# One quarter of an MLP's first activation moved to Pool, four instead of two banks of its second activation on the vector engine

## The reference

```python
f   = lrelu(conv(x, sw1)); f = lrelu(conv(f, sw2)); f = conv(f, sw3)      # 16 features
h   = lrelu(conv(concat[f, pts[d]], mw1) + mb1)     # 17 -> 32
h   = lrelu(conv(h, mw2) + mb2)                     # 32 -> 32
h   = lrelu(conv(h, mw3) + mb3)                     # 32 -> 16
sdf = sigmoid(conv(h, mw4) + mb4)                   # 16 -> 1
x   = x1 + sdf
```

## Time and profile before

| | us |
|---|---|
| median of 3 runs | 9322.48 |
| lowest and highest | 9307.45, 9324.88 |
| span of the profiled execution | 9326.0 |
| PE, DVE, ACT, POOL busy | 8848.9, 8762.5, 8085.3, 5789.8 |

### The profile page before, as it was taken

The page is one execution under the profiler, slowest core; times in us unless marked ns, Lnnn a source line. Parts: engine busy times, 40 slices in busy tenths (PEclk is TensorE's granted clock), DMA queues, the critical chain, the costliest instruction groups (busy, mean ns, idle before and its releaser), DMA issues. The chain is left out here.

```text
span 9326.0 us, 448546 instructions
## 1 busy us (share of the span) xinstructions
PE 8848.9 (95%) x199690; PEld 3696.6 (40%) x199690; DVE 8762.5 (94%) x9984; ACT 8085.3 (87%) x12777; POOL 5789.8 (62%) x2583
## 2 busy tenths in 40 slices
PE   7999999999999999999999999899999999999999
PEld 4555555555555555555555555311111111111111
DVE  6999999999999999999999999899999999999998
ACT  6888888888887888888888888699999999999999
POOL 6999999999999999999999999400000000000000
PEclk9999999999999999999999999899999999999999
DMA  4333333333333333333333333211111111111110
GB/s 116 98 94 90 85 82 87 99 99 95 85 83 83 96 94 96 86 88 77 87 88 83 87 84 82 58 32 32 34 34 32 32 31 32 34 32 32 34 34 19
DMA packets 394249, 638.98 MB, mean 69 GB/s; under 512 B 98016, under 2 KB 98626, under 8 KB 391810
## 3 DMA queue, kind: packets, MB, share of 16 engines
q1 hardware_dynamic: 389184, 608.56, 25.1%
q10 hardware_dynamic: 2498, 0.95, 0.0%
q0 software_dynamic: 640, 0.77, 0.0%
HBM read 270.15 MB, written 71.30 MB: 37 GB/s over the span
## 5 line engine op out<-in xcount | busy, mean ns | idle before, releaser
L1087 DVE TENSOR_TENSOR_SCAN arena<-arena,carried,ps 128x512 f32<-128x512 f32 x3968 | 4758.3, 1260 | 284.9 <-PE ps L505 271.4
L934 POOL TENSOR_TENSOR arena<-arena 128x1024 f32<-128x1024 f32 x2048 | 4799.9, 2394 | 89.8 <-PE ps L516 35.4
L1152 DVE SCALAR_TENSOR_TENSOR arena<-arena,neg_p 128x512 f32<-128x512 f32 x4096 | 2748.1, 744 | 0.1
L804 ACT ACTIVATE arena<-arena,a_neg 128x512 f32<-128x512 f32 x4096 | 2662.3, 710 | 15.7 <-DVE arena L1087 8.9
L505 PE MATMUL ps<-arena 64*32 64x128 f32 x131072 | 2306.2, 275 | 71.9 <-DVE arena L1087 41.7
L505 PEld LDWEIGHTS ps<-arena 64*32 64x32 f32 x131072 | 1848.2, 106 | 1197.1 <-DVE arena L1087 666.4
L873 ACT ACTIVATE arena<-ps,b2t 128x1024 f32<-128x1024 f32 (+1 forms) x2048 | 2076.2, 1077 | 201.1 <-PE ps L637 193.7
L637 PE MATMUL ps<-arena,w2s 32*32 32x512 f32 x32768 | 1549.3, 600 | 115.2 <-ACT arena L873 102.9
L879 ACT ACTIVATE arena<-ps,bm 128x1024 f32<-128x1024 f32 x1024 | 1165.6, 1138 | 2.0 <-PE ps L648 2.0
L648 PE MATMUL ps<-arena,m 64*32 64x512 f32 x16384 | 1127.4, 600 | 3.3 <-ACT arena L879 0.9
L516 PE MATMUL ps<-arena,sel 128*32 128x512 f32 x8192 | 1012.1, 611 | 66.5 <-POOL arena L934 60.9
(11 more groups left out here) (138 smaller groups left out, 5738.2 us busy)
## 6 DMA issues: line engine op xcount, KB each, us to landing
arena<-arena SPq DMA_DIRECT2D x4096, 64.0 KB, 2.4
arena<-c_d SPq DMA_DIRECT2D x1024, 128.0 KB, 3.3
xr<-in_x SPq DMA_DIRECT2D x128, 256.0 KB, 3.2
x_d<-xr SPq DMA_DIRECT2D x128, 256.0 KB, 3.3
xs<-x_d SPq DMA_DIRECT2D x128, 256.0 KB, 4.2
xr<-x_d SPq DMA_DIRECT2D x128, 256.0 KB, 3.7
out<-arena SPq DMA_DIRECT2D x128, 256.0 KB, 2.4
xs<-in_x SPq DMA_DIRECT2D x96, 256.0 KB, 3.2
```

The lines of the kernel that those rows point to most:

```text
L804: A(dA[(UNITS * t + m) % DR][:, gi, :], drep[:, e, :], ACT.Exp, scale=a_neg[:, e, 2 * gp + gi:2 * gp + gi + 1]).then_inc(s_dA, 1)
L934: nc.gpsimd.tensor_tensor(hc[m % CR], H[:, m % HR, :, :], crep[:, 2 * gp:2 * gp + 2, :], ALU.mult).then_inc(s_ch, 1)
L1087: V.tensor_tensor_scan(H[:, m % HR, gi, :], dA[(UNITS * t + m) % DR][:, gi, :], dbu[m % 2].rearrange("p (l g) -> p g l", g=2)[:, gi, :], 0 ...
L1152: m = V.scalar_tensor_tensor(out=t1[k % 4][:, q, :], in0=g[par], scalar=neg_p[:, i:i + 1], in1=gs_[par], op0=ALU.max, op1=ALU.add)
```

## The change

In each step, the t1 tile of q = 3 is made by Pool in place of DVE. Pool does it with two instructions: a tensor_scalar (min with the largest finite float, which changes nothing, then max with -p) from g into one of two new tiles `top`, and a tensor_tensor that adds gs into t1. Pool writes them in the order maximum(j), add_slope(j - 1). maximum(j) waits for the end of add_slope(j - 2), which stands just ahead of it in the queue; add_slope waits for its maximum and for the t1 buffer. mm2 waits for Pool's semaphore as well. SHARED grows from (1, 3) to (0, 2, 4, 6): DVE makes bank 3 of the second activation in four steps of eight and ACT in the other four. The loop of DVE in `leaky1` shrinks from four to three instructions, and `spread_g` waits for Pool's last use of the g and gs buffers.

```diff
-SHARED = (1, 3)
+SHARED = (0, 2, 4, 6)
+HUGE = 3.4028234663852886e38
...
+        top = [over(50 + i, 1) for i in range(2)]
...
-        pool_counts = {s_du: 1, s_dg: 2, s_ch: UNITS}
+        pool_counts = {s_du: 1, s_dg: 2, s_ch: UNITS, s_top: NG, s_l1p: NG}
...
             def mm2(t, k):
                 pe.wait_ge(s_l1, t * NG + (k + 1))
+                pe.wait_ge(s_l1p, t * NG + (k + 1))
...
+            def maximum(n, k):
+                t, s, par = n + 1, n // 4 + 1, n // 4 % 2
+                pool.wait_ge(s_l1p, t * NG + k - 1)
+                if n % 4 == 0 and k == 0:
+                    pool.wait_ge(s_g, s + 1)
+                i = GQ * (NG * (n % 4) + k) + GQ - 1
+                nc.gpsimd.tensor_scalar(top[k % 2], g[par], HUGE, neg_p[:, i:i + 1], ALU.min, ALU.max).then_inc(s_top, 1)
+
+            def add_slope(n, k):
+                t, par = n + 1, n // 4 % 2
+                pool.wait_ge(s_top, t * NG + k + 1)
+                pool.wait_ge(s_m2, t * (2 * NG) + 2 * (k - 3))
+                nc.gpsimd.tensor_tensor(t1[k % 4][:, GQ - 1, :], top[k % 2], gs_[par], ALU.add).then_inc(s_l1p, 1)
...
             for n in range(0, NT):
                 layer0(n)
+            for j in range(NG * NT + 1):
+                if j < NG * NT:
+                    maximum(j // NG, j % NG)
+                if j > 0:
+                    add_slope((j - 1) // NG, (j - 1) % NG)
...
             def spread_g(s, par):
 
                 dve.wait_ge(s_gp, s + 1)
+                if s > 2:
+                    dve.wait_ge(s_l1p, NG * (4 * (s - 2) + 1))
...
-                for q in range(GQ):
+                for q in range(GQ - 1):
```

More of the change, by code:

```diff
@@ L197, in mamba_sdf_kernel @@
         s_l1, s_m2 = sem("s_h1"), sem("s_mm2")
+        s_top, s_l1p = sem("s_h1_maximum_by_pool"), sem("s_h1_by_pool")
         s_t2, s_m3 = sem("s_h2"), sem("s_mm3")
```

## The result

The changed kernel takes 10,250.7 us (10,248.0 to 10,252.7, 4 runs) against 9323.4 us before. The ratio is 1.0997, 95% interval 1.0983 to 1.1011. The loss is 927 us where 1267 us were predicted.

The account below looks back on a forecast made before the run. It took PE, DVE and ACT, coupled in layer 1 at 3.265 us a step, as the bound. DVE 2.43 plus Pool 2.00 gave 4.43, 4.5 with wake-ups; times 1024 steps, 1265 us more, 10,590 us; range 10,130 to 11,250.

Parts of the forecast that it names:

- What bounds the kernel: Layer 1, 3.265 us a step: PE, DVE and ACT coupled; relieving one gains a few per cent, no more.
- Removed and added: Layer 1, per block of 8 steps: DVE nets 2.4 us freed of 26.1, ACT loses 0.84 us; PE keeps its matmuls.
- Exclusion: Layer 1: DVE instructions with two SBUF operands and Pool instructions reading SBUF exclude each other; 4.43 us a step.
- A run keeps the other out: From layer 0's trace: a back-to-back Pool run holds DVE out for the whole run, 4.07 us, not one instruction's 2.39.
- The sum: Layer 1 step: DVE 2.43 plus Pool 2.00 makes 4.43 us, 4.5 by the two-step walk; 10,590 us, 13.6% slower.
- wake-ups: Layer 1: restart delays of Pool, PE and DVE, estimated at 0.35 us in all for two steps.
- Pool's pair: Layer 1, each step: Pool's tensor_scalar 0.80 us and tensor_tensor 1.20 us, together 2.0 us.
- a walk: Two steps of layer 1: DVE burst 4.7, Pool pair 2.0, mm2 and L1161 1.95, 0.35 more: 9.0 us.
- The fast rival: Layer 1: long DVE and Pool instructions stream side by side, ACT sets the pace; middle 9,170 us; chance 0.05.
- Pool far slower: Layer 1: Pool's min-max takes 2.4 us, making the step 6.0 us, 12,150 us; chance 0.06.
- The clock: Layer 1: longer PE gaps drop the clock to 1.2 GHz, PE's work doubles to 5.4 us, 11,510 us; chance 0.04.
- Signs listed: Layer 1: 4.5 us steps, single L1152 of 2 us and more, longer Pool instructions, PE at 7 tenths, L1161 waiting longer.

Follow-up runs that it names:

- e12: Changed kernel with g read from its PSUM bank, first two feature layers in mm4's bank, SHARED back to (1, 3): 9349.2 us, ratio 1.0022 to before.
- e10: Kernel before with g read from its PSUM bank and first two feature layers in mm4's bank, no Pool work: 9331.0 us, ratio 1.0004.
- e2: Kernel before with only SHARED changed to (0, 2, 4, 6), Pool doing nothing in layer 1: 9578.2 us, ratio 1.027.
- e1: Changed kernel with SHARED put back to (1, 3), Pool still making its quarter: 9914.6 us, ratio 1.0632 to before.
- e3: Kernel before, DVE making all four tiles, with Pool's two instructions a step added into scratch tiles nobody reads: 10,632.5 us, ratio 1.1405.
- e4: As e3, with Pool's two instructions replaced by two memsets that only write SBUF: 9326.0 us, ratio 1.0 to before.
- e6: Changed kernel with features computed once, for the first four blocks, and g in SBUF: 10,185.7 us, ratio 1.0924 to before.
- e7: As e6, but DVE's first-activation instruction reads g from PSUM instead of SBUF: 9098.5 us, ratio 0.9756 to before.
- e9: Changed kernel, whole computation, g read from its PSUM bank by DVE, first two feature layers in mm4's bank: 9254.2 us, ratio 0.9926 to before.

## Why the prediction came out as it did

**What bounds the kernel.** Borne out by e12 against e10, and by e2: DVE, ACT and PE run in one period. Taking DVE's load away alone gains nothing, adding to it costs 250 us.

**Removed and added.** DVE's spacing of 0.662 us and its account per step held: e1 and e2 came within 35 and 18 us of sums made from it (for e1 with the 1.33 us shut out, taken from the result).

**Exclusion.** Right, and shown: e3 against e4 for Pool's reads, e6 against e7 for DVE's second SBUF operand. The single-column instructions of the earlier trace rows were enough to foretell it. The trace has all six of the layer 0 cases, 4.07 to 6.20 us, that the prediction took from their medians.

**A run keeps the other out.** This step was wrong for layer 1. There DVE waits for one Pool instruction at a time. The longest L1177 in the changed kernel is 1.847 us, one Pool sum (1.28) plus DVE's own 0.54, and none waits for a pair. In layer 0 a Pool instruction starts before the one ahead of it has ended (four in 9.29 us, with a mean of 2.394), and DVE waits for the run. It would be natural to lay this on gaps, since in layer 1 Pool's min-max starts 0.10 us behind the end of the sum, for whose semaphore it waits. The trace of the changed kernel speaks against that:

```profile
7970.67 1.00 POOL L987 TENSOR_SCALAR arena<-arena,neg_p 128x512 f32<-128x512 f32 x1
7971.64 1.71 POOL L993 TENSOR_TENSOR arena<-arena 128x512 f32<-128x512 f32 x1
```

```profile
7971.04 1.17 DVE L1177 SCALAR_TENSOR_TENSOR arena<-arena,neg_p 128x512 f32<-128x512 f32 x1
```

The sum starts 0.03 us before the min-max ahead of it ends (7971.67), and DVE's instruction has been waiting. DVE still has its turn first: it ends at 7972.21, 0.54 us behind the min-max, and the sum 1.14 us after that. From 6000 us on, Pool's sum starts before its min-max has ended 211 times, and in all 211 a DVE instruction gets in between. So two Pool instructions without a gap are not enough to keep DVE out. Layer 0 also differs in the columns (1024), in what follows what (two-operand instructions in a row) and in DVE's own instruction (one column). Which of these makes the run hold, no run shows, and it stays open.

**The sum.** Predicted 4.43 us a step excluded and 4.5 with wake-ups; measured 4.17. Four terms were mis-sized:
- Pool's pair was put at 0.80 + 1.20 us. Undisturbed it is 0.69 + 1.28 us, nearly the same sum of 1.97. But only 0.56 + 1.14 = 1.70 us of it shuts DVE out, 0.30 us less.
- DVE's instruction was counted with its whole spacing of 0.662 us; behind a Pool instruction it needs only 0.54 us more. With two turns a step that saves 0.24 us.
- L1161 and the copies were put at nothing, since they lie beside Pool's work. That step was wrong for more than half of them. L1186 and the copies are 0.41 us of DVE's time a step. Of L1186's 364 us in the window only 158 us pass while Pool has an instruction, and none of the copies' 41 us; 0.25 us a step stay.
- The 0.35 us of wake-ups for two steps hung on a walk in which DVE waits for Pool through mm2. It doesn't: DVE waits at L1186 for 56 us in 4100, 0.06 us a step, and Pool waits 1131 us for mm2, since it runs ahead until its t1 buffers are full.

With these the prediction's sum is 4.43 - 0.30 - 0.24 + 0.25 + 0.06 = 4.20 us, against 4.17 measured. The errors pull against each other, and that the forecast came within 3.2% owes something to this luck. Counted from DVE's side it is the same: 2.84 us of its own and at most 0.43 behind the min-max and 1.02 behind the sum are 4.29 us, and what Pool does beside L1186 brings it to 4.17.

**The fast rival** did not come for this code. It was found in e7 and e9, where its condition (side by side) holds for the first activation. **Pool far slower**: no, its min-max takes 0.69 us. GPSIMD Engine Reference, section 3.1, in the Trainium skill, would give 0.77 us for its best loop; here the min-max with two operations is a little faster, 0.69 us in e12. **The clock**: in the changed kernel the mean granted clock of the window is 0.91 where it was 1.00. It is made of short stretches at the lower level (0.50), 813 us of layer 1's 4289 us, with PE waiting more than before. It did not set the end, as PE waits 624 us for DVE and ACT, and DVE's lengthened instructions account for the step by themselves. e6 has 722 us at the lower level and e7 none, so the clock came back when the exclusion went.

**Signs listed.** DVE looks busy and Pool's instructions lengthen, as said. Single L1177 instructions reach 1.85 us, not 2 and more. PE stands at 8 tenths, not 7, and waits for DVE's L1186, not for Pool's add. L1186 does not wait longer for mm2 but less, 56 us in 4100 where L1161 waited 135 us in 3200. The undisturbed min-max of 0.69 us lies inside the stated 0.6 to 1.2 us.

## What to carry to other kernels

Before work goes to Pool, count how many SBUF operands the vector engine's instructions beside it have. Two on DVE and a read on Pool made one queue of the two engines here, and then the moved work cost more than it relieved. Look for a tiny DVE instruction that already runs beside Pool: if its duration jumps from 0.2 to 4 us, that is the queue. It does not tell how long a turn is between long instructions: there DVE waited for one Pool instruction, not for a run. One operand left in PSUM opened the queue here, and the relief paid only once it was spent on ACT's banks.

## What was not expected of the hardware

- The exclusion covers less than an instruction takes: 0.54 us of a spacing of 0.662 for DVE's two-operand instruction on 512 columns, 0.56 us of 0.69 for Pool's min-max, 1.14 us of 1.28 for Pool's sum.
- The time shut out is counted as busy. DVE shows 98% and 95% with the same instruction at 1.151 and 0.744 us; the mean duration tells what the busy share hides.
- Two Pool instructions without a gap between them let a waiting DVE instruction in, 211 times of 211 in layer 1, while the runs of layer 0 did not, six times of six.
- Pool's min-max with a column operand, 0.69 us for 128x512, is hardly slower than DVE's 0.66 us spacing for its two-operand instruction.
